# Scores and maxima of an attention stage in four row groups of 32 rows, with the division moved behind the attention

## The chip, the cores and the metric

One core of one Trainium2 chip. The metric is the device time of the whole program in microseconds. The median of three runs of the kernel before is 2633.51 us (2630.73 to 2633.67).

## What is computed

A transformer block with conditioning: x is (2, 2048, 512), 16 heads of 32, MLP width 1024, all in float32. Cut to what matters:

```python
ada = silu(c) @ Wada + bada          # shift, scale and gate for both halves
h = ln(x) * (1 + scale_msa) + shift_msa
q, k, v = h @ Wq + bq, h @ Wk + bk, h @ Wv + bv      # 16 heads of 32
A = softmax(q k^T / sqrt(32))
x = x + gate_msa * ((A v) @ Wo + bo)
h2 = ln(x) * (1 + scale_mlp) + shift_mlp
return x + gate_mlp * (gelu(h2 @ W1 + b1) @ W2 + b2)
```

## The kernel before

Three stages. Stage 1 (to 357 us) makes queries, keys and values in eight chunks of 512 rows. Each query and key is split in two reduced-precision float32 numbers, high and low, and stored in DRAM (q_hi, q_lo, k_hi, k_lo). Stage 3 (from 2180 us) does output projection, norm and MLP in eight blocks of 512 rows; block 0's projection is already done inside the last head.

Stage 2 is the attention: 32 heads g (2 batches of 16), each with 16 key tiles t of 128 keys and four query chunks j of 512 queries. PSUM has eight banks. Per head:

- *Max scores* for head g+1 (max_scores, L1104): 64 matmuls of 96 rows (high and low products below each other) with queries as weights, into three banks in turn. VectorE reduces each to one maximum per query (find_max, L868), then all partial ones (L812); TensorE turns them (transpose_max, L1047), VectorE negates (L818), and one DMA (put_max, L391) lays them as row 96 of the head's queries. Row 96 of the keys is one.
- *Scores* for head g (scores, L1113): 64 matmuls of 97 rows, into three banks in turn. ScalarE takes the exponential of each (probs, L670) into `prob`, a ring of four key tiles.
- *Values* (L1127): for each key tile four matmuls in four column groups of 32, one per query chunk; a float32 matmul is two passes, so eight stand in the trace.
- *Denominators*: GpSimd adds eleven of the sixteen tiles of `prob` in halves (sum_probs, L538, 20 additions), and TensorE sums the other five tiles and GpSimd's result over the partitions (L1118), all accumulated in one bank of its own. ScalarE copies output and denominator (L645, L650); VectorE inverts 128x512 denominators (L874) and multiplies the head's output (L877); SP stores it (store_head, L398).

Each engine runs its own list in order. TensorE's order in a step is: scores of chunks 0 and 1 with max scores between, then the sum of tile t-2 where TensorE has it, values of tile t-1, then scores of chunks 2 and 3 with max scores between. SP's order for head g (stage2, L401) is: load_head for head g+2 (seven DMAs of 256 KB: three pieces of queries, three of keys, values), put_max for head g+1, store_head of head g-1. Buffers of queries, keys, values are three deep. The loop body has three heads. In head 0, twelve weight pieces for stage 3 are loaded and split besides (late, L426, L639, L882). In the last head (31) there are no max scores; block 0 of the attention is loaded in two halves (load_first_oT), split by ScalarE (L689) and VectorE (L896), and projected (first_projection).

In stage 3 a block's attention is loaded (load_oT), split (split_oT, oT_rest) and projected during the block before it (project, after the first of eight mlp2).

## Time and profile before

| | us |
|---|---|
| median of three runs | 2633.51 |
| profiled execution, first to last instruction | 2625.2 |
| TensorE matmuls busy | 2543.3 (97%) |
| weight loads busy (beside the matmuls) | 1482.7 (56%) |
| VectorE busy | 1841.4 (70%) |
| GpSimd busy | 1625.0 (62%) |
| ScalarE busy | 1309.9 (50%) |
| mean granted TensorE clock | 0.989 |
| DMA, mean over the span | 62 GB/s |

A matmul's busy time contains its way through the array, so matmuls overlap in the trace: what one costs is the distance between two starts. PE are matmuls, PEld weight loads, DVE VectorE, ACT ScalarE, POOL GpSimd, SPq SP's queue. "x8" joins neighbours of one kind; in brackets stands the engine's idle time before a row and what ended it. In a row of a stretch the columns are length, busy time with count for PE, PEld, DVE, ACT and POOL, then TensorE's granted clock, DMA share and GB/s.

### The profile page before, as it was taken

The numbers are of one execution on the slowest core, as the hardware profiler recorded it, in microseconds if no ns is written. First come the engines' busy times: TensorE is split into PE (matmuls) and PEld (weight loads), VectorE is DVE, ScalarE is ACT, GpSimd is POOL, SyncE is SP. The second block draws the span as 40 slices with busy tenths as digits, with TensorE's granted clock in tenths as the row PEclk, the third lists the DMA queues.
The fourth block names the chain that finished last, engine by engine and source line by source line (L and its number), as shares of the span: only waits on it lengthen the run. The fifth ranks groups of instructions, "written<-read, shape, count | busy, mean of one in ns | idle before, by whom it ended". The sixth has DMA issues, their size and how long they took to land.

```text
span 2625.2 us, 45742 instructions
## 1 busy us (share of the span) xinstructions
PE 2543.3 (97%) x13208; PEld 1482.7 (56%) x13208; DVE 1841.4 (70%) x2872; ACT 1309.9 (50%) x2429; POOL 1625.0 (62%) x744
## 2 busy tenths in 40 slices
PE   7999899999999999999999999999999979999998
PEld 5788654444444444444444444444444437888887
...
DMA packets 141459, 163.15 MB, mean 62 GB/s; under 512 B 76048, under 2 KB 92944, under 8 KB 134032
## 3 DMA queue, kind: packets, MB, share of 16 engines
...
q14 instruction: 130, 1.06, 0.1%
...
## 4 chain that ended last, share of the span: by engine, by line
PE 93%; DVE 3%; issue 1%; ACT 1%; DMA 1%; SPq 0%; POOL 0%; ACTq 0%; POOLq 0%; DVEq 0%
PE ps L1113 21%; PE ps L1015 20%; PE ps L1104 19%; PE ps L1127 18%; PE ps L1118 7%; PE ps L1248 7%; DVE part_max L868 1%; PE ps L1024 1%; DVE weights_r L882 1%; PE ps L1059 1%; PE ps L1047 0%; DMA work<-v_rows 0%; DVE work L942 0%; ACT work L670 0%; DMA work<-in_x 0%
## 5 line engine op out<-in xcount | busy, mean ns | idle before, releaser
L538 POOL TENSOR_TENSOR work<-work 128x1024 f32<-128x1024 f32 x640 | 1505.7, 2395 | 296.7 <-PE ps L1118 262.7
L868 DVE TENSOR_REDUCE part_max<-ps 128x1 f32<-128x512 f32 x1984 | 1229.0, 682 | 321.3 <-PE ps L1104 320.7
L670 ACT ACTIVATE work<-ps 128x512 f32<-128x512 f32 x2048 | 1070.9, 602 | 697.3 <-PE ps L1113 697.2
L1113 PE MATMUL ps<-acts_r 97*128 97x512 f32 x2048 | 836.4, 418 | 26.0 <-ACT work L670 14.7
L1104 PE MATMUL ps<-acts_r 96*128 96x512 f32 x1984 | 811.3, 409 | 6.8 <-DVE part_max L868 6.7
L1113 PEld LDWEIGHTS ps<-acts_r 97*128 97x128 f32 x2048 | 383.1, 190 | 396.7 <-ACT work L670 308.4
L1127 PE MATMUL ps<-work 128*32 128x512 f32 x4096 | 545.3, 604 | 0.0
L1104 PEld LDWEIGHTS ps<-acts_r 96*128 96x128 f32 x1984 | 375.6, 189 | 263.0 <-DVE part_max L868 182.4
L1015 PE MATMUL ps<-acts_r,weights_r 128*128 128x512 f32 x1536 | 380.3, 397 | 5.7 <-DVE acts_r L790 5.7
L1015 PEld LDWEIGHTS ps<-acts_r,weights_r 128*128 128x128 f32 x1536 | 291.1, 191 | 69.3 <-issue 6.8
L547 POOL TENSOR_TENSOR work<-work,gate_b 128x512 f32<-128x512 f32 x60 | 84.5, 1439 | 214.3 <-DMA work<-in_x 172.8
L1127 PEld LDWEIGHTS ps<-work 128*32 128x32 f32 x4096 | 94.2, 109 | 203.2 <-issue 186.6
L1118 PE MATMUL ps<-work,ones 128*32 128x512 f32 x1536 | 206.4, 610 | 0.0
L505 POOL TENSOR_TENSOR var_eps<-var_eps,mv 128x4 f32<-128x4 f32 x16 | 3.2, 201 | 327.2 <-DVE mv L768 327.2
L713 ACT ACTIVATE work<-ps,b_sb 128x512 f32<-128x512 f32 x64 | 44.1, 690 | 309.7 <-PE ps L1015 309.6
L1248 PE MATMUL ps<-w_r,acts_r 128*128 128x512 f32 x768 | 184.5, 391 | 0.0
L1015 PE MATMUL ps<-weights_r,acts_r 128*128 128x512 f32 x768 | 183.6, 392 | 0.0
L1015 PEld LDWEIGHTS ps<-weights_r,acts_r 128*128 128x128 f32 x768 | 143.7, 188 | 36.9 <-issue 7.0
L1248 PEld LDWEIGHTS ps<-w_r,acts_r 128*128 128x128 f32 x768 | 143.0, 188 | 29.2 <-issue 0.2
L607 ACT ACTIVATE work<-ps,bq_sb 128x512 fp32r<-128x512 f32 x64 | 44.1, 689 | 206.3 <-PE ps L1015 170.9
L922 DVE CAST acts_r<-work 128x512 fp32r<-128x512 f32 x64 | 27.9, 436 | 128.6 <-ACT work L713 128.6
L874 DVE RECIPROCAL bv_rows<-bv_rows 128x512 f32<-128x512 f32 x32 | 106.6, 3331 | 8.0 <-ACT bv_rows L650 8.0
...
## 6 DMA issues: line engine op xcount, KB each, us to landing
work<-in_x SPq DMA_DIRECT2D x16, 1024.0 KB, 5.4
acts_r<-q_hi SPq DMA_DIRECT2D x64, 256.0 KB, 4.8
acts_r<-k_hi SPq DMA_DIRECT2D x64, 256.0 KB, 6.4
q_hi<-work SPq DMA_DIRECT2D x32, 256.0 KB, 2.6
q_lo<-work SPq DMA_DIRECT2D x32, 256.0 KB, 3.3
k_hi<-work SPq DMA_DIRECT2D x32, 256.0 KB, 2.6
k_lo<-work SPq DMA_DIRECT2D x32, 256.0 KB, 3.2
v_rows<-work SPq DMA_DIRECT2D x32, 256.0 KB, 2.0
```

Source lines behind the costliest of these rows:

```text
L538: nc.gpsimd.tensor_tensor(psum_acc[:, at], first, prob[:, t % RING, at], ALU.add).then_inc(add_ok, 1)
L547: nc.gpsimd.tensor_tensor(xc[b][:, t, :], xc[b][:, t, :], gate_b[:, which, b, :], ALU.add).then_inc(done, 1)
L607: nc.scalar.activation(qk_st[:, m % 2, 0, :].bitcast(F32R), ps[:, 2 + m % 4, :], ACT.Identity, bias=bq_sb[:, m // KC, m % KC:m % KC + 1]). ...
L670: nc.scalar.activation(prob[:, t % RING, j * CH:(j + 1) * CH], ps[:, A_BANKS + (u + t * NQ + j) % B_BANKS, :], ACT.Exp, scale=SCALE).then_ ...
L868: nc.vector.tensor_reduce(part_max[:, f // NQ, f % NQ:f % NQ + 1], ps[:, (u + f) % A_BANKS, :], AX.X, ALU.max).then_inc(a_max, 1)
L874: nc.vector.reciprocal(recip[:], recip[:]).then_inc(rec_ok, 1)
L1015: mm = nc.tensor.matmul(o, lhs(s, kk), rhs(r, kk), start=(kk == 0 and s == r), stop=(kk == KC - 1 and s == 1))
L1104: nc.tensor.matmul(ps[:, (u + f) % A_BANKS, :], qs[u][0:M_ROW, f // NQ * P:(f // NQ + 1) * P], ks[u][0:M_ROW, j * CH:(j + 1) * CH], start= ...
L1113: nc.tensor.matmul(ps[:, A_BANKS + (u + t * NQ + j) % B_BANKS, :], ks[u][0:M_ROW + 1, t * P:(t + 1) * P], qs[u][0:M_ROW + 1, j * CH:(j + 1 ...
L1118: mm = nc.tensor.matmul(ps[j * DH:(j + 1) * DH, DEN_BANK, :], ones[:, 0:DH], src(j), start=first, stop=last)
L1127: mm = nc.tensor.matmul(ps[j * DH:(j + 1) * DH, O_BANK, :], v_sb[u][:, t, :], prob[:, t % RING, j * CH:(j + 1) * CH], start=(t == 0), stop ...
L1248: mm = nc.tensor.matmul(ps[:, 4 + t, :], g_r[:, f % 4, s, t * P:(t + 1) * P], w2_r[:, r, f, :], start=(f == 0 and s == r), stop=(f == FB - ...
```

## The change

- Queries and keys are loaded four times, once for each group of 32 partitions: high and low parts of the keys in full (four DMAs of 256 KB each), of the queries one chunk for each group (four of 64 KB each). High parts are three buffers deep, low parts and values two. SP's order for head g is now: high parts of head g+2; the store of a sum; low parts and values of head g+1; store_head; stores of sums, the load of all sums, the store of the reciprocals, and put_max between them.
- A max score multiplies high parts only, 32 rows. A step's four stand in row groups 2, 3, 0, 1. They run two steps ahead of the head (LEAD), so the maxima of head g+1 are complete after step 13 of head g. Head 0 has two steps' worth more.
- A score of chunk r is four accumulating matmuls in row group r and bank 3+r: high by high, low by high, high by low, and a row of minus ones by the row of maxima. The chunks' parts are interleaved.
- The maxima are turned by VectorE in 32x32 squares and laid into one row per group by 16 DMAs; TensorE waits for them before the first tile's last part.
- GpSimd adds ten tiles. The six other tiles and GpSimd's result are summed over partitions each into a max bank; ScalarE copies each into one buffer `sums`, SP stores it. The seven are loaded back spread over all partitions, VectorE adds and inverts them (128x16), SP stores the reciprocals.
- The head's output is stored undivided. At the output projection the reciprocals are loaded (16 DMAs a block) and multiplied on: by VectorE for block 0, by GpSimd for the others.
- The last block of w2 is loaded and split in the last head, since its place holds queries before. The loop body has six heads, the loop four rounds, and heads 25 to 30 stand unrolled.

```diff
--- before.py
+++ after.py
@@ constants @@
-NBUF = 3
+HI_BUF, TWO = 3, 2
+PERIOD = 6
-POOL_TILES = [0, 1, 2, 3, 5, 6, 7, 9, 10, 11, 12]
+POOL_TILES = [0, 1, 3, 4, 6, 7, 9, 10, 12, 13]
+ND = len(PE_TILES) + 1
+EXPS = 4
+LEAD = 2
+EXTRA_AT = (3, 8)
+A_BANKS, S_BANK, O_BANK = 3, 3, 7
+LOADS_HI, LOADS_LO, LOADS_0 = 8, 9, 6
+MAX_PIECES = 4
...
@@ def _(sp): @@
+            def load_k(dst, src, g, done):
+                for r in range(NQ):
+                    sp.dma_start(dst[r * DH:(r + 1) * DH, :].bitcast(F32), src[1][bass.ds(g * DH, DH), :]).then_inc(done, 16)
+            def load_q(dst, src, g, done):
+                for r in range(NQ):
+                    sp.dma_start(dst[r * DH:(r + 1) * DH, :].bitcast(F32), src[0][bass.ds(g * DH, DH), r * CH:(r + 1) * CH]).then_inc(done, 16)
+            def load_hi(g, u):
+                load_q(q_hi[u], qk_hi, g, hi_in[u])
+                load_k(k_hi[u], qk_hi, g, hi_in[u])
...
+                for w in range(MAX_PIECES):
+                    for r in range(NQ):
+                        row = m_row[u][r * DH:r * DH + 1, :].bitcast(F32).rearrange("o (s q) -> o s q", q=P)
+                        sp.dma_start(row[:, :, w * DH:(w + 1) * DH],
+                                     max_T[w * DH + r * TT:w * DH + (r + 1) * TT, :]).then_inc(maxT_in, 16)
...
+            def store_sums(i, g, uses):
+                for d, _, _, n in uses:
+                    n = i * (PERIOD * ND) + n
+                    sp.wait_ge(sums_ok, n)
+                    sp.dma_start(sums_dram[bass.ds(g * ND + d, 1), :].rearrange("o (r q) -> (o r) q", q=CH), sums[0:P:DH, :]).then_inc(sums_out, 16)
+            def load_sums(g):
+                sp.wait_ge(sums_out, 16 * ND * (g + 1))
+                sp.dma_start(sums_c[:], sums_dram[bass.ds(g * ND, ND), :].rearrange("n (p x) -> p n x", x=NT)).then_inc(sums_in, 16)
+            def store_rec(g):
+                sp.wait_ge(rec_ok, g + 1)
+                sp.dma_start(rec_dram[bass.ds(g, 1), :].rearrange("o (p x) -> (o p) x", x=NT), rec_c[:]).then_inc(rec_out, 16)
...
+                if loads:
+                    sp.wait_ge(b_mm, g * FILLS)
+                    load_hi(g + 2, (k + 2) % HI_BUF)
+                sums_of((0,))
+                if load_next:
+                    sp.wait_ge(pv_mm, START + g * NT)
+                    sp.wait_ge(b_mm, g * FILLS)
+                    load_lo(g + 1, (k + 1) % TWO)
+                    load_v(g + 1, (k + 1) % TWO)
+                store_head(g - 1, (k - 1) % TWO)
+                sums_of(range(1, 5))
+                load_sums(g - 1)
+                sums_of(range(5, 9))
+                store_rec(g - 1)
+                sums_of(range(9, NT - 1))
+                if load_next:
+                    put_max(g + 1, (k + 1) % TWO)
+                sums_of((NT - 1,))
...
+            sp.wait_ge(a_max, FILLS)
+            load_q(q_hi[0], qk_hi, 0, hi_in[0])
             put_max(0, 0)
-            store_v(NCHUNK - 1, *ORDER[NCHUNK - 1], range(2, TT))
+            load_hi(1, 1)
...
+            def load_rec(b, c, dst):
+                for k in range(KC):
+                    for r in range(NQ):
+                        src = rec_dram[bass.ds(b * H + c * NQ, NQ), k * CH + r * P:k * CH + (r + 1) * P]
+                        src = src.rearrange("g (o q) -> o g q", o=1).broadcast_to((DH, NQ, P))
+                        sp.dma_start(dst[k][r * DH:(r + 1) * DH, :].rearrange("d (g q) -> d g q", q=P), src).then_inc(rec_in, 16)
...
+            sp.wait_ge(oT_ok, 2)
+            sp.dma_start(w2_st, w2[FF - P:FF, :]).then_inc(w2_last_in, 16)
+            load_sums(G - 2)
...
+            load_sums(G - 1)
+            store_rec(G - 1)
+            sp.wait_ge(rec_out, 16 * G)
+            load_rec(1, 0, rec)
...
@@ def _(pool): @@
+                pool.wait_ge(rec_in, (n + 1) * (16 * KC * NQ))
+                pool.wait_ge(oT_in, n * 16 + 32)
+                for blk in range(KC):
+                    nc.gpsimd.tensor_tensor(oTf[:, blk, :], oTf[:, blk, :], rec[blk], ALU.mult).then_inc(oT_ok, 1)
...
@@ def _(act): @@
+            def take_sums(i, g, uses):
+                for d, bank, _, n in uses:
+                    if d < ND - 1:
+                        act.wait_ge(pv_mm, START + g * NT + PE_TILES[d] + 1)
+                    else:
+                        act.wait_ge(den_mm, START + g + 1)
+                    if n > 1:
+                        act.wait_ge(sums_out, 16 * (i * (PERIOD * ND) + n - 1))
+                    nc.scalar.activation(sums, ps[:, bank, :], ACT.Copy).then_inc(sums_ok, 1)
...
@@ def _(dve): @@
+            def transpose_max(g):
+                dve.wait_ge(max_ok, g + 1)
+                if not isinstance(g, int) or g:
+                    dve.wait_ge(maxT_in, g * (16 * MAX_PIECES))
+                nc.vector.transpose(max_T[:], row_max[:]).then_inc(maxT_ok, 1)
...
+            def denominators(g):
+                dve.wait_ge(sums_in, 16 * (g + 1))
+                if not isinstance(g, int) or g:
+                    dve.wait_ge(rec_out, 16 * g)
+                nc.vector.tensor_reduce(den_c[:], sums_c[:].rearrange("p n x -> p x n"), AX.X, ALU.add).then_inc(den_ok, 1)
+                dve.wait_ge(den_ok, g + 1)
+                nc.vector.reciprocal(rec_c[:], den_c[:]).then_inc(rec_ok, 1)
...
+            def normalise_first(half):
+                dve.wait_ge(oT_in, 16 * half + 16)
+                if half == 0:
+                    dve.wait_ge(rec_in, 16 * KC * NQ)
+                for k in range(2):
+                    nc.vector.tensor_tensor(tmp3[:, k, :], tmp3[:, k, :], rec0[:, 2 * half + k, :], ALU.mult).then_inc(oT_ok, 1)
...
@@ def _(pe): @@
+            def bank_free(i, before):
+                if before:
+                    kind, n = before
+                    if kind == "M":
+                        pe.wait_ge(a_max, i * (PERIOD * FILLS) + n)
+                    else:
+                        pe.wait_ge(sums_ok, i * (PERIOD * ND) + n)
+            def max_tile(i, u, q, r, use):
+                bank, before, _ = use
+                bank_free(i, before)
+                at = slice(r * DH, (r + 1) * DH)
+                nc.tensor.matmul(ps[:, bank, :], q_hi[u][at, q // NQ * P:(q // NQ + 1) * P],
+                                 k_hi[u][at, q % NQ * CH:(q % NQ + 1) * CH], start=True, stop=True).then_inc(a_mm, 1)
+            def score_part(i, k, t, r, part):
+                g, u, w = i * PERIOD + k, k % HI_BUF, k % TWO
+                if part == 0 and (t or k):
+                    pe.wait_ge(exp_ok, START + g * (NT * EXPS) + t * EXPS + r - EXPS + 1)
+                if part == 3 and t == 0:
+                    pe.wait_ge(maxT_in, (g + 1) * (16 * MAX_PIECES * NQ))
+                at = slice(r * DH, (r + 1) * DH)
+                keys = slice(t * P, (t + 1) * P)
+                o = ps[:, S_BANK + r, :]
+                if part == 0:
+                    nc.tensor.matmul(o, k_hi[u][at, keys], q_hi[u][at, :], start=True, stop=False)
+                elif part == 1:
+                    nc.tensor.matmul(o, k_lo[w][at, keys], q_hi[u][at, :], start=False, stop=False)
+                elif part == 2:
+                    nc.tensor.matmul(o, k_hi[u][at, keys], q_lo[w][at, :], start=False, stop=False)
+                else:
+                    row = slice(r * DH, r * DH + 1)
+                    nc.tensor.matmul(o, minus_r[row, :], m_row[w][row, :], start=False, stop=True).then_inc(b_mm, 1)
...
+            def take_sums(i, k, uses):
+                for d, bank, before, _ in uses:
+                    bank_free(i, before)
+                    if d < ND - 1:
+                        sums_of(lambda j: prob[:, PE_TILES[d] % RING, j * CH:(j + 1) * CH], bank).then_inc(pv_mm, 1)
+                    else:
+                        pe.wait_ge(add_ok, START + (i * PERIOD + k + 1) * (NADD * HALVES))
+                        sums_of(lambda j: psum_acc[:, j * CH:(j + 1) * CH], bank).then_inc(den_mm, 1)
...
+                for t, step in enumerate(A_USES[k]):
+                    ahead = 1 + q // per_head
+                    u = (k + ahead) % HI_BUF
+                    if step["max"] and (k == 0 and t == 0 or q == per_head):
+                        pe.wait_ge(hi_in[u], (nth(i, k + ahead, HI_BUF) + 1) * (16 * LOADS_HI))
+                    if step["extra"]:
+                        for r, use in zip((2, 3, 0, 1), step["extra"]):
+                            max_tile(i, u, q % per_head, r, use)
+                        q += 1
+                    score_part(i, k, t, 0, 0)
+                    score_part(i, k, t, 1, 0)
+                    for r, use in zip((2, 3), step["max"][:2]):
+                        max_tile(i, u, q % per_head, r, use)
+                    for part in range(1, 4):
+                        score_part(i, k, t, 0, part)
+                        score_part(i, k, t, 1, part)
+                        score_part(i, k, t, 2, part - 1)
+                        score_part(i, k, t, 3, part - 1)
+                    for r, use in zip((0, 1), step["max"][2:]):
+                        max_tile(i, u, q % per_head, r, use)
+                    score_part(i, k, t, 2, 3)
+                    score_part(i, k, t, 3, 3)
+                    if step["max"]:
+                        q += 1
+                    if t:
+                        values(i, k, t - 1)
+                    elif k:
+                        values(i, k - 1, NT - 1)
+                    take_sums(i, k if t > 1 else k - 1, step["sums"])
                     if t in between:
                         between[t]()
```

## Rows read from the trace of the kernel before

**Rows 1.** The page: TensorE's share, and the chain that ended last by line
```profile
PE 2543.3 (97%) x13208; PEld 1482.7 (56%) x13208; DVE 1841.4 (70%) x2872; ACT 1309.9 (50%) x2429; POOL 1625.0 (62%) x744
...
PE ps L1113 21%; PE ps L1015 20%; PE ps L1104 19%; PE ps L1127 18%; PE ps L1118 7%; PE ps L1248 7%; DVE part_max L868 1%; PE ps L1024 1%; DVE weights_r L882 1%; PE ps L1059 1%; PE ps L1047 0%; DMA work<-v_rows 0%; DVE work L942 0%; ACT work L670 0%; DMA work<-in_x 0%
```
**Rows 2.** Groups by line (line, engine, form, count, busy us, mean ns)
```profile
L874 DVE RECIPROCAL bv_rows<-bv_rows 128x512 f32<-128x512 f32 x32 | 106.6, 3331 | 8.0 <-ACT bv_rows L650 8.0
...
L547 POOL TENSOR_TENSOR work<-work,gate_b 128x512 f32<-128x512 f32 x60 | 84.5, 1439 | 214.3 <-DMA work<-in_x 172.8 <-DVE work L773 41.4
...
L818 DVE TENSOR_SCALAR neg_max<-ps 16x128 fp32r<-16x128 f32 x32 | 8.9, 279 | 22.8 <-PE ps L1047 22.8
```
**Rows 3.** SP's queue, put_max (L391): start us, us; heads 1, 31; all 32
```profile
422.67 0.52 SPq L391 DMA_DIRECT2D acts_r<-neg_max  x1
...
2088.83 0.52 SPq L391 DMA_DIRECT2D acts_r<-neg_max  x1
...
L391 SPq DMA_DIRECT2D acts_r<-neg_max x32: 512/518/621, 354.3 to 2088.8; - x32
...
DMA to landing us min/median/max: 1.8/1.8/1.9
```
**Rows 4.** Timeline of TensorE, one step and a step's start (start us, us, what)
```profile
1055.29 1.06 PE L1127 MATMUL ps<-work 128*32 128x512 f32 x8
...
1056.62 0.40 PE L1104 MATMUL ps<-acts_r 96*128 96x512 f32 x1
...
1058.03 0.40 PE L1104 MATMUL ps<-acts_r 96*128 96x512 f32 x1
1058.36 1.06 PE L1118 MATMUL ps<-work,ones 128*32 128x512 f32 x8
1059.24 1.04 PE L1127 MATMUL ps<-work 128*32 128x512 f32 x8
```
**Rows 5.** SP's queue, one head's output stores
```profile
1037.28 1.89 SPq L398 DMA_DIRECT2D attention_T<-work  x4
```
**Rows 6.** Timelines: VectorE and GpSimd in a middle head, ScalarE in the last head
```profile
1053.52 3.08 DVE L868 TENSOR_REDUCE part_max<-ps 128x1 f32<-128x512 f32 x5 [0.34 <-PE ps L1104]
...
1042.95 47.06 POOL L538 TENSOR_TENSOR work<-work 128x1024 f32<-128x1024 f32 x20 [8.07 <-PE ps L1118]
...
2159.47 2.06 ACT L670 ACTIVATE work<-ps 128x512 f32<-128x512 f32 x4 [0.60 <-PE ps L1113]
```
**Rows 7.** Timeline of weight loads (PEld): into column groups, and full width
```profile
1055.29 0.16 PEld L1127 LDWEIGHTS ps<-work 128*32 128x32 f32 x8 [0.24 <-issue]
...
100.29 0.53 PEld L1003 LDWEIGHTS ps<-tmp 128*128 128x128 f32 x4
```
**Rows 8.** A stretch with a head's loads (last three: PEclk, DMA share, GB/s)
```profile
1044.00:1052.00 8.00, 8.00 (x44) 4.40 (x42) 6.88 (x12) 6.17 (x13) 7.87 (x4) 1.00 1.05 214
```
**Rows 9.** DMA issues: count, KB each, median us from issue to landing
```profile
work<-in_wada SPq DMA_DIRECT2D x5, 1024.0 KB, 5.6
...
gate<-in_wv SPq DMA_DIRECT2D x1, 1024.0 KB, 14.6
...
bv_rows<-in_bv SPq DMA_DIRECT2D x1, 256.0 KB, 12.3
```
**Rows 10.** TensorE after a wait, the stretch behind it, and twelve us of the last head
```profile
379.46 0.50 PE L1104 MATMUL ps<-acts_r 96*128 96x512 f32 x1 [1.40 <-DVE part_max L868]
...
380.60:384.00 3.40, 3.40 (x16) 1.29 (x19) 3.40 (x3) 1.83 (x4) 3.34 (x3) 0.50 0.13 49
2148.00:2160.00 12.00, 11.02 (x55) 3.80 (x51) 1.44 (x7) 8.79 (x18) 11.21 (x7) 1.00 0.00 0
```
**Rows 11.** TensorE's first matmul of head 0
```profile
357.48 0.47 PE L1113 MATMUL ps<-acts_r 97*128 97x512 f32 x1 [0.83 <-issue]
```
**Rows 12.** A wait in the last head; first MLP matmuls; block 1's projection
```profile
ACT acts_r L689 <- DMA tmp<-attention_T: 11.1, 1, 11.1
...
2180.10 8.45 PE L1015 MATMUL ps<-acts_r,weights_r 128*128 128x512 f32 x36 [1.83 <-DVE acts_r L790]
...
2193.92 3.34 PE L1015 MATMUL ps<-weights_r,acts_r 128*128 128x512 f32 x14
```

More of the change, by code:

```diff
@@ L124, in block_kernel @@
         gf = view(work, 3584, 2, CH)
+        rec = [view(work, at, CH) for at in (2560, 3072, 4608, 5120)]
         assert STEP_ROOT in POOL_TILES
@@ L430, in _ @@
                     stored(NCHUNK)
-                    load_head(2, 2)
+                    load_v(1, 1)
+                    load_hi(2, 2)
+                    load_lo(1, 1)
+            for t in range(len(late), NT - 1):
+                store_sums(0, 0, A_USES[0][t]["sums"])
             put_max(1, 1)
-            with sp.Fori(0, G // NBUF - 1) as i:
-                for k in range(1, NBUF + 1):
-                    stage2(i * NBUF + k, k % NBUF, True)
+            store_sums(0, 0, A_USES[0][NT - 1]["sums"])
+            with sp.Fori(0, ROUNDS) as i:
+                for k in range(1, PERIOD + 1):
+                    head(i, k)
             def heads_stored(n):
-                for u in range(NBUF):
-                    sp.wait_ge(o_out[u], START + 16 * NQ * len(range(u, n, NBUF)))
+                for u in range(TWO):
+                    sp.wait_ge(o_out[u], START + 16 * NQ * len(range(u, n, TWO)))
             def rows_oT(b, c):
@@ L1117, in denominators, with sums_of, values @@
+            def sums_of(src, bank):
                 for j in range(NQ):
-                    mm = nc.tensor.matmul(ps[j * DH:(j + 1) * DH, DEN_BANK, :], ones[:, 0:DH], src(j), start=first, stop=last)
+                    mm = nc.tensor.matmul(ps[j * DH:(j + 1) * DH, bank, :], ones[:, 0:DH], src(j), start=True, stop=True)
                 return mm
-            def values(g, u, t):
-                pe.wait_ge(exp_ok, START + g * (NT * NQ) + (t + 1) * NQ)
-                if t == 0 and not (isinstance(g, int) and g == 0):
+            def values(i, k, t):
+                g = i * PERIOD + k
+                pe.wait_ge(exp_ok, START + g * (NT * EXPS) + (t + 1) * EXPS)
+                if t == 0 and k:
@@ L1190, in _ @@
             pe.wait_ge(v_ok, START + NCHUNK * TT)
[L1191 to L1192 removed]
+            pe.wait_ge(a_max, FILLS)
+            pe.wait_ge(hi_in[0], 16 * LOADS_HI)
+            head(0, 0)
             nc.disable_value_cache = True
[L1194 to L1197 removed]
+            with pe.Fori(0, ROUNDS) as i:
+                for k in range(1, PERIOD + 1):
+                    head(i, k)
@@ L1198, in _ @@
             nc.disable_value_cache = False
+            for g in range(AFTER, G - 1):
+                head(0, g)
             def project_tile(n, t):
```

420 lines of the change are left out of this document (226 added, 194 removed).

## Prediction

> **What bounds the kernel now.** I read the page's shares first, then its groups by line, then single steps of the timeline. TensorE is busy 97% of the span, and three of its lines in the attention stage are most of the chain that ended last: scores (L1113) 21%, max scores (L1104) 19%, values (L1127) 18% [rows 1]. (L1015, the products of the other stages, isn't touched.) The queue's put_max rows give the time of a head: (2088.83 - 422.67)/30 = 55.5 us [rows 3]. A step of a head is seen in [rows 4]: eight 512-column score or max matmuls, one each 0.233 us, then the values. From one values group to the next are 3.07 us, so all that is not those eight costs 3.07 - 8 x 0.233 = 1.20; a step that also sums its tile (L1118) costs 0.88 more. A head is 128 x 0.233 + 16 x 1.20 + 6 x 0.88 = 54.4 of the 55.5 us. The other engines have room: per 55.5 us a head costs VectorE 64 maxima at 0.62 (five stand in 3.08) = 39.7 and 3.3 of reciprocal, ScalarE 64 exponentials at 0.49 (four in 2.06) = 31.4, GpSimd 20 additions in 47.1 [rows 2, 6].
>
> **What the change takes off TensorE.** A max score of 96 rows becomes one of 32; four stand in four row groups and four banks. A score becomes four accumulating parts (high x high, low x high, high x low, minus the maximum), each in its own row group. If four row groups work at the same time, a step has five rounds in place of eight matmuls. The trace before has no row groups. The nearest rows are the values: eight passes into four column groups, each shown as about 0.6 us, are through in 1.0 us, and their eight weight loads begin within 0.16 us [rows 4, 7]. I take full overlap, a round at 0.233 (upper bound: none at all, 4 x 0.233). Then TensorE's own work is 80 x 0.233 + 19.2 + 7 x 0.88 = 44.0 us a head, 10.4 less. The Trainium skill ("TensorEngine Tiling (Array Packing)", Key Properties) says that different tiles load weights and multiply in parallel, which would be this value.
>
> GpSimd goes from 20 additions to 18 (42.4 us); VectorE loses the reciprocal of 3.3 and keeps 39.7. ScalarE copies seven sums and one output, 8 x 0.49, 35.3 in all. None of these is above 44. What sets the head is who waits for whom:
>
> **1. The four score banks.** Bank r of step t+1 must wait for exponential r of step t, and the third and fourth row group enter a round after the first two; the TensorE queue is in order, so the first bank's last two parts stand behind the fourth bank's first. After the fourth exponential: 0.16 to the matmul, one round, then 0.43 until the exponential starts. Before, in the last head, which has no max scores, the same kind of loop shows as four exponentials in 2.07 and 0.60 idle [rows 6]. Here it is 2.07 + 0.16 + 0.233 + 0.43 = 2.90 us for a step without a sum (9 of them). A step with a sum (7) is TensorE's: 5 x 0.233 + 1.20 + 0.88 = 3.25. Together 26.1 + 22.8 = 48.9 us. After a sum, a max matmul waits for its copy (the sums use the max banks): 0.5 a head in step 1.
>
> **2. The maximum's way to its row.** Removed: one transpose on TensorE, one negation, one DMA. Added: a VectorE transpose and 16 DMAs. SP issues one each 0.46 us (four in 1.89), and one such DMA lands 1.8 us after its issue [rows 3, 5]. The search runs two steps ahead: the last maximum is reduced about 2.2 us into step 13's later rounds, maxima and transpose (the negation's 0.28 [rows 2] as its price; the transpose is in no row) end at 2.75, and the row is complete at 2.75 + 0.1 + 15 x 0.46 + 1.8 + 0.2 = 11.75. The first bank's last part of the next head is due at 2.90 + 2.90 + 3.25 + 0.23 = 9.28. TensorE stands 2.5 us each head, with values, sums and max scores queued behind that wait.
>
> **3. The partial sums' way out.** ScalarE has one buffer for them, so a copy waits until the last store has landed. The store after step 1 stands in SP's queue behind load_lo and load_v (9 issues) and store_head (4), and on the rings behind their data. A head loads 2.8 MB where it loaded 1.8; the 8 us stretch of a head load shows 214 GB/s [rows 8], so high and low parts take 12 us, values and output 3. Counted from step 14, the high parts are issued from 7.9 and their data run to 15; the row of maxima is there at 8.7; the low parts are issued from 13.3 (after step 0's sum), their data and the values' run to 23, the output's and the store's to 24.5; step 3's copy wants it at 21.8 and the exponentials of step 4 queue behind it. That is 2.4 us, or 1.6 after point 4 has moved the copy later. Whether a small store waits behind bulk is seen in the start of the kernel: 1 MB loads issued close behind each other land 5.6 us after their issue (median of five) and then 14.6, and the smaller one issued behind them after 12.3 [rows 9]. At the low bound (1.8 us, as put_max alone) this wait is zero.
>
> **4. TensorE's clock.** In the trace before, a stand of 1.40 us (at 378) is soon followed by 3.4 us at a granted clock of 0.50 (1.2 GHz in place of 2.4) [rows 10]. The last head's steps, 11.02 us busy of 12, kept 1.00 [rows 10], and the new steps' stands are no longer than theirs. The waits of points 2 and 3 are as long, so I expect two such stretches a head: in steps 0 and 1, which TensorE sets, half of 3.4 = 1.7 us; in steps 4 and 5, which have 0.9 us of room each, about 1.1. Low bound 0.
>
> A head: 48.9 + 0.5 + 2.5 + 1.7 + 1.6 + 1.1 = 56.3 us, 0.8 more than before; times 30 = +23 us. TensorE's gain of 10.4 goes into waits: its saving is real and all of it is spent.
>
> **5. The two ends.** Start: head 0 may begin only with head 1's keys. SP issues 4 query loads, then 16 for the maximum (found at about 354.3, when put_max was issued before [rows 3]), then 8 more: 354.5 + 24 x 0.46 = 365.5, and some 4.5 us for the last 256 KB to land, 370 against 357.5 [rows 11]; with a slow clock behind it +14.5. Last head: its first block of attention is divided on VectorE before ScalarE may split it (ScalarE stands 11.1 us for that block already [rows 12]) +3; w2's last piece is split between step 8's exponentials and the residual, +4; 12 steps at 2.90 in place of 2.67 +3; x's norm waits one tile longer +1. Block 1's projection began 13.8 us after the first MLP matmul (2193.92 - 2180.10) [rows 12]; now the last sum must be copied (0.6), stored (2.3), loaded spread over the partitions (3.5, more packets), added and inverted (0.5), stored (2.3), and 16 loads issued and landed (9.2), multiplied on GpSimd (four at 1.44 [rows 2]) and split (1.2): about 26 us. +12 and 2 of slow clock. The later blocks' divisions are loaded a block ahead and lie beside TensorE's work; uncovered, each would cost 5.8. Ends: +39.5 us.
>
> **The sum.** The profiled run is 2625.2 us, the median 2633.5, 8.3 more (I add that). 2633.5 + 23 + 39.5 = 2696 us.
>
> **Rivals.** *Shorter waits (faster than before).* If the small stores are not held by the bulk, point 3 and its slow stretch go: 53.6 a head, 30 x -1.9 = -57, 2616. If short stands do not lower the clock either, 51.9 a head: 30 x -3.6 = -108, 2565. For it: put_max's 1.8 us [rows 3], and that the load of before has room between its bursts; against: the landings of [rows 9] and the clock of [rows 10]. It decides at 54.2 us a head, where 30 heads pay for the ends. Chance 0.26.
> *Row groups share the weight load.* Full-width loads one behind the other take 0.53 us for four, 0.11 from start to start [rows 7]. If the four row groups take turns at it, a round is 0.45: steps of 3.45 and 4.33, 61.4 a head, the row of maxima waits 0.7, the clock stays: 62.5, 30 x 7 = +210, 2883. A round of 0.30 would give 51.8 + 0.5 + 2.1 + 1.7 + 1.3 + 1.0 = 58.4, 30 x 2.9 = +87, 2760. Its mechanism is the same, a part of the overlap missing; for it: no row shows row groups; against: the eight loads within 0.16. Chance 0.20 for both. The Trainium skill ("TensorE: Matmul & The Clock Gate", Measured speedup vs the span model) has four tiles of 32 rows at 3.07 times one after another; an estimate from that is 4 x 0.233/3.07 = 0.30.
> *It does not overlap at all.* 20 x 0.233 + 1.20 a step: 100 us a head, near 4000. Chance 0.03.
> *My forecast* of two waits a head holds 0.51, with its own range 2650 to 2745 (an issue of 0.37 or 0.56 instead of 0.46 moves 15 issues by 1.5 us).
> The Trainium skill ("TensorEngine Tiling (Array Packing)", PSUM Bottleneck) says tiling speeds up the matmuls and not what empties PSUM. Point 1 agrees with it by rows: the exponentials' loop sets nine steps of 16.
>
> **Numbers.** 0.2% (5 us) is about what a measurement can tell. Faster by more: 0.26 from the short waits and 0.01 = 0.27. Within: 0.05, between the cases. Slower: 0.68. The range goes from the short-wait case's middle to the partly overlapping rounds and above, 2580 to 2840.
>
> **What would show it.** Right: heads of 56 us; max and score matmuls of 32 rows starting four together, rounds 0.23 apart; four exponentials in 2.07, 0.8 idle; at step 0 TensorE stands 2 to 3 us for the max row's DMA; ScalarE's third sums copy waits for a DMA; PEclk under 1 in the slices of the stage; TensorE idle 12 us before head 0 and before block 1's projection. Wrong: rounds further apart than 0.3, no DMA wait ahead of step 0, a sums store that lands in 2 us behind load_v, or heads under 54.2 us.

## The result: 11% slower, and the profile after

The kernel after takes 2918.3 us (median of four runs, 2914.9 to 2922.0) against 2632.7 for the kernel before, a ratio of 1.109 (interval 1.107 to 1.111). The forecast was 2696, in a range up to 2840: the sign was right, the size far off. The profiled run spans 2919.5 us, 294.3 more than before.

The page of the kernel after (shares; chain by engine and by line; three groups: line, engine, operation, count | busy us, mean ns | idle before):

```profile
PE 2552.5 (87%) x19544; PEld 1366.5 (47%) x19544; DVE 1756.7 (60%) x2878; ACT 1420.8 (49%) x2622; POOL 1505.1 (52%) x706
...
PE 63%; SPq 21%; DMA 5%; issue 4%; DVE 4%; ACT 3%; POOL 0%; ACTq 0%; DVEq 0%; POOLq 0%
PE ps L1245 17%; PE ps L1374 13%; SPq L489 9%; PE ps L1353 7%; SPq L496 6%; PE ps L1490 6%; PE ps L1364 5%; PE ps L1339 4%; PE ps L1355 3%; PE ps L1360 3%; PE ps L1357 2%; SPq L470 2%; SPq L466 2%; DMA partial_sums<-work 2%; DVE part_max L1069 2%
...
L1360 PE MATMUL ps<-acts_r,minus_r 1*128 1x512 f32 x1024 | 240.9, 470 | 65.0 <-DMA acts_r<-max_T 65.0
L1360 PE MATMUL ps<-m_odd,minus_r 1*128 1x512 f32 x1024 | 234.6, 460 | 57.3 <-DMA m_odd<-max_T 57.3
...
L838 ACT ACTIVATE work<-ps 128x512 f32<-128x512 f32 x224 | 133.9, 598 | 224.9 <-DMA partial_sums<-work 166.8
```

Before, three TensorE lines made up most of the chain [rows 1]. Now 21% of it is SP's queue: the row of maxima (L489, put_max) has 9%, the output stores (L496, store_head) 6%, loads (L466, L470) and small stores the rest. The two waits at the right are the two places the prediction named: TensorE at the row of maxima (122 us in all) and ScalarE's copies at the stores of the sums (167 us).

Where the 294.3 us are, by the same landmarks as in [rows 3, 11, 12]. TensorE's start of head 0, the first put_max in head 0, the one 30 heads later, the first MLP matmul and block 1's projection after:

```profile
375.12 0.79 PE L1353 MATMUL ps<-acts_r 32*128 32x512 f32 x2 [18.56 <-DVE work L1002]
...
453.92 2.49 SPq L489 DMA_DIRECT2D m_odd<-max_T  x4
...
2353.76 0.61 SPq L489 DMA_DIRECT2D m_odd<-max_T  x1
...
2458.68 8.47 PE L1245 MATMUL ps<-acts_r,weights_r 128*128 128x512 f32 x36 [1.38 <-ACT work L838]
...
2485.20 2.07 PE L1245 MATMUL ps<-weights_r,acts_r 128*128 128x512 f32 x4 [12.54 <-DVE acts_r L1121]
```

| stretch | before | after | more | forecast |
|---|---|---|---|---|
| to the first matmul of head 0 | 357.5 | 375.1 | +17.6 | +14.5 |
| from there to the first put_max | 65.2 | 78.8 | +13.6 | 0 |
| 30 heads: (2353.76 - 453.92)/30 = 63.3 each | 1666.2 | 1899.8 | +233.7 | +23 |
| to the first MLP matmul | 91.3 | 104.9 | +13.6 | +11 |
| to block 1's projection | 13.8 | 26.5 | +12.7 | +14 |
| the rest | | | +3.1 | 0 |

The ends are nearly as forecast; the heads are not. One head of the kernel after on SP's queue (start, length from first to last of the joined issues), then ScalarE in the same head. L858 are the exponentials, L838 copies of sums, L827 the output; step 0 starts at 1034.60:

```profile
1022.78 9.91 SPq L489 DMA_DIRECT2D acts_r<-max_T  x16
1032.97 0.59 SPq L504 DMA_DIRECT2D partial_sums<-work  x1
1033.85 1.92 SPq L470 DMA_DIRECT2D acts_r<-q_hi  x4
1035.86 2.76 SPq L466 DMA_DIRECT2D acts_r<-k_hi  x4
1040.12 0.61 SPq L504 DMA_DIRECT2D partial_sums<-work  x1
1041.32 1.71 SPq L470 DMA_DIRECT2D acts_r<-q_lo  x4
1043.12 1.77 SPq L466 DMA_DIRECT2D acts_r<-k_lo  x4
1045.09 0.40 SPq L477 DMA_DIRECT2D work<-v_rows  x1
1045.69 6.22 SPq L496 DMA_DIRECT2D attention_T<-work  x4
1052.18 3.08 SPq L504 DMA_DIRECT2D partial_sums<-work  x2
```

```profile
1034.60 2.06 ACT L858 ACTIVATE work<-ps 128x512 f32<-128x512 f32 x4 [5.34 <-PE ps L1360]
...
1046.80 2.06 ACT L858 ACTIVATE work<-ps 128x512 f32<-128x512 f32 x4 [0.82 <-PE ps L1360]
1053.95 0.60 ACT L838 ACTIVATE work<-ps 128x512 f32<-128x512 f32 x1 [5.08 <-DMA partial_sums<-work]
1054.44 2.19 ACT L858 ACTIVATE work<-ps 128x512 f32<-128x512 f32 x4
1059.39 2.06 ACT L858 ACTIVATE work<-ps 128x512 f32<-128x512 f32 x4 [2.76 <-PE ps L1360]
1062.48 2.06 ACT L858 ACTIVATE work<-ps 128x512 f32<-128x512 f32 x4 [1.02 <-PE ps L1360]
1065.05 0.60 ACT L838 ACTIVATE work<-ps 128x512 f32<-128x512 f32 x1 [0.51 <-PE ps L1364]
1066.06 2.07 ACT L858 ACTIVATE work<-ps 128x512 f32<-128x512 f32 x4 [0.41 <-PE ps L1360]
1068.96 2.07 ACT L858 ACTIVATE work<-ps 128x512 f32<-128x512 f32 x4 [0.84 <-PE ps L1360]
1071.85 2.07 ACT L858 ACTIVATE work<-ps 128x512 f32<-128x512 f32 x4 [0.82 <-PE ps L1360]
```

Undisturbed steps (from 1066) are the forecast's: 2.90 us, four exponentials in 2.07, idle 0.8. The two stands (stretches in which an engine waits), 5.34 and 5.08 us, are not. TensorE, the rounds of such a step, and the granted clock after each stand (last columns: PEclk, DMA share, GB/s):

```profile
1065.16 0.40 PE L1355 MATMUL ps<-acts_r 32*128 32x512 f32 x2
1065.17 0.40 PE L1353 MATMUL ps<-acts_r 32*128 32x512 f32 x2
...
1065.63 0.39 PE L1360 MATMUL ps<-acts_r,minus_r 1*128 1x512 f32 x2
1065.64 0.40 PE L1357 MATMUL ps<-w_r,acts_r 32*128 32x512 f32 x2
```

```profile
1033.60:1040.40 6.80, 6.63 (x40) 2.94 (x44) 2.16 (x4) 3.15 (x6) 0.00 (x0) 0.50 0.67 169
...
1053.90:1061.00 7.10, 6.40 (x40) 2.39 (x40) 3.76 (x6) 4.27 (x9) 4.68 (x2) 0.52 0.08 9
```

Four matmuls in four row groups start within 0.01 us, and 1065.16 to 1065.63 are two rounds, 0.23 each. The four groups overlap in full. Behind both stands of this head the clock is 0.50, the 1.2 GHz level, for about 6.8 us. It isn't always so long. From the first exponential of head 1 to that of head 31, 64 stretches at 0.50 begin in the trace, 39 of 6.8 us and 25 of 3.4. A stand of 4.35 us at the row of maxima, as long as the one before 1033.77, has 3.4 us behind it here:

```profile
780.38 0.59 PE L1360 MATMUL ps<-acts_r,minus_r 1*128 1x512 f32 x2 [4.35 <-DMA acts_r<-max_T]
...
781.00:784.40 3.40, 3.40 (x20) 0.85 (x18) 1.29 (x2) 1.98 (x4) 0.00 (x0) 0.50 0.46 121
784.40:787.80 3.40, 3.31 (x40) 1.39 (x36) 2.39 (x4) 2.79 (x6) 0.00 (x0) 1.00 1.02 243
```

### The profile page after: what moved, and what is told of

Its sections match the earlier page's. It is cut to its first block, busy times and chain, and to the rows that moved or that the text cites. A ratio compares the mean times of both kernels' runs of the same rounds, so it can differ in the third digit from the quotient of the medians.

```text
span 2919.5 us, 59447 instructions
## 1 busy us (share of the span) xinstructions
PE 2552.5 (87%) x19544; PEld 1366.5 (47%) x19544; DVE 1756.7 (60%) x2878; ACT 1420.8 (49%) x2622; POOL 1505.1 (52%) x706
## 4 chain that ended last, share of the span: by engine, by line
PE 63%; SPq 21%; DMA 5%; issue 4%; DVE 4%; ACT 3%; POOL 0%; ACTq 0%; DVEq 0%; POOLq 0%
PE ps L1245 17%; PE ps L1374 13%; SPq L489 9%; PE ps L1353 7%; SPq L496 6%; PE ps L1490 6%; PE ps L1364 5%; PE ps L1339 4%; PE ps L1355 3%; PE ps L1360 3%; PE ps L1357 2%; SPq L470 2%; SPq L466 2%; DMA partial_sums<-work 2%; DVE part_max L1069 2%
## 5 line engine op out<-in xcount | busy, mean ns | idle before, releaser
L710 POOL TENSOR_TENSOR work<-work 128x1024 f32<-128x1024 f32 x576 | 1352.8, 2386 | 784.5 <-PE ps L1364 431.5
L858 ACT ACTIVATE work<-ps 128x512 f32<-128x512 f32 x2048 | 1060.0, 603 | 563.1 <-PE ps L1360 561.9
L1374 PE MATMUL ps<-work 128*32 128x512 f32 x4096 | 613.4, 674 | 0.0
L1339 PE MATMUL ps<-acts_r 32*128 32x512 f32 x1344 | 397.6, 503 | 103.9 <-ACT work L838 85.9
L1353 PE MATMUL ps<-acts_r 32*128 32x512 f32 x1408 | 357.3, 494 | 33.8 <-DVE work L1002 18.6
L1353 PEld LDWEIGHTS ps<-acts_r 32*128 32x128 f32 x1408 | 154.8, 198 | 414.7 <-ACT work L858 340.6
L1355 PE MATMUL ps<-acts_r 32*128 32x512 f32 x1408 | 310.0, 431 | 0.0
L1360 PE MATMUL ps<-acts_r,minus_r 1*128 1x512 f32 x1024 | 240.9, 470 | 65.0 <-DMA acts_r<-max_T 65.0
L1360 PE MATMUL ps<-m_odd,minus_r 1*128 1x512 f32 x1024 | 234.6, 460 | 57.3 <-DMA m_odd<-max_T 57.3
L1339 PEld LDWEIGHTS ps<-acts_r 32*128 32x128 f32 x1344 | 186.6, 197 | 181.3 <-ACT work L838 105.1
L1364 PE MATMUL ps<-work,ones 128*32 128x512 f32 x1792 | 257.9, 651 | 0.0
L838 ACT ACTIVATE work<-ps 128x512 f32<-128x512 f32 x224 | 133.9, 598 | 224.9 <-DMA partial_sums<-work 166.8
L1339 PE MATMUL ps<-acts_r,w_r 32*128 32x512 f32 x640 | 187.5, 506 | 44.5 <-ACT work L838 42.5
L1357 PE MATMUL ps<-w_r,acts_r 32*128 32x512 f32 x1024 | 218.1, 446 | 0.0
L1357 PE MATMUL ps<-acts_r 32*128 32x512 f32 x1024 | 215.1, 442 | 0.0
```

The lines of the kernel that those rows point to most:

```text
L710: nc.gpsimd.tensor_tensor(psum_acc[:, at], first, prob[:, t % RING, at], ALU.add).then_inc(add_ok, 1)
L858: nc.scalar.activation(prob[:, t % RING, j * CH:(j + 1) * CH], ps[:, S_BANK + j, :], ACT.Exp, scale=SCALE).then_inc(exp_ok, 1)
L1339: nc.tensor.matmul(ps[:, bank, :], q_hi[u][at, q // NQ * P:(q // NQ + 1) * P], k_hi[u][at, q % NQ * CH:(q % NQ + 1) * CH], start=True, sto ...
L1353: nc.tensor.matmul(o, k_hi[u][at, keys], q_hi[u][at, :], start=True, stop=False)
L1355: nc.tensor.matmul(o, k_lo[w][at, keys], q_hi[u][at, :], start=False, stop=False)
L1357: nc.tensor.matmul(o, k_hi[u][at, keys], q_lo[w][at, :], start=False, stop=False)
```

## The experiments

All times are medians of four runs. For each kernel the steps of a head are given as the time from the first exponential of a step to that of the next, mean over heads 1 to 30 of its profiled run; steps 5 to 14 differ little and only one kind stands here.

| kernel | us | step 15 | 0 | 1 | 2 | 3 | 4 | later, no sum | head | head 0 |
|---|---|---|---|---|---|---|---|---|---|---|
| after | 2918.3 | 8.31 | 5.49 | 3.87 | 3.09 | 7.08 | 4.64 | 2.91 | 63.3 | 87.3 |
| e1_max4 | 2757.1 | 3.77 | 3.92 | 6.32 | 4.19 | 5.50 | 3.50 | 2.91 | 58.2 | 84.4 |
| e2_lead4 | 2842.1 | 6.10 | 4.64 | 4.86 | 3.43 | 6.42 | 4.18 | 2.91 | 60.5 | 86.2 |
| e3_values_later | 2791.1 | 8.38 | 5.49 | 3.90 | 3.15 | 4.42 | 3.30 | 2.91 | 59.3 | 87.7 |
| e4_sums_first | 2750.9 | 8.36 | 5.57 | 3.72 | 2.96 | 3.51 | 2.91 | 2.91 | 57.7 | 87.2 |
| e5_both | 2670.1 | 3.73 | 3.78 | 6.36 | 4.26 | 3.68 | 2.91 | 2.91 | 55.4 | 84.4 |
| e6_spread | 2552.5 | 3.78 | 3.97 | 3.77 | 2.97 | 3.46 | 2.91 | 2.91 | 51.6 | 87.3 |
| e7_lag | 2592.3 | 3.87 | 3.89 | 3.78 | 3.02 | 3.58 | 2.95 | 2.96 | 52.6 | 88.6 |
| e9_max_last | 2545.3 | 3.78 | 3.74 | 3.77 | 2.97 | 3.44 | 2.91 | 2.91 | 51.3 | 84.2 |
| e8_lag_max_last | 2535.2 | 3.81 | 3.69 | 3.77 | 2.97 | 3.45 | 2.71 | 2.73, 2.90 | 50.9 | 81.6 |
| e10_split_later | 2535.0 | 3.74 | 3.70 | 3.78 | 2.94 | 3.44 | 2.91 | 2.91 | 51.3 | 73.0 |
| e11_all | 2530.4 | 3.89 | 3.79 | 3.76 | 2.97 | 3.44 | 2.72 | 2.73, 2.90 | 51.0 | 75.7 |

The kernel before has 55.5 and 67.6 in the last two columns. The theory at the start: the 7.8 us a head are two waits on SP's queue, each with its slow clock. The rivals: the loads' data, or a cost of the row groups themselves.

**Row of maxima by 4 DMAs.**

```diff
-for r in range(NQ):
-    row = m_row[u][r * DH:r * DH + 1, :]...
-    sp.dma_start(row[:, :, w * DH:(w + 1) * DH], max_T[w * DH + r * TT:w * DH + (r + 1) * TT, :])
+rows = m_row[u][0:P:DH, :].bitcast(F32).rearrange("r (s q) -> r s q", q=P)
+sp.dma_start(rows[:, :, w * DH:(w + 1) * DH], max_T[w * DH:w * DH + NT, :])
```

> The row of maxima is laid by 4 DMAs (four rows each) in place of 16. Theory (a head of the changed kernel is 50.0 us of steps, a stand of 4.9 for this row at step 0, 2.7 for the slow clock behind it, 4.2 for ScalarE's copy in step 3 and 2.2 for the slow clock behind that): 12 issues of 0.62 us less, the stand at step 0 and its slow clock go, the second wait stays. 56 us a head in place of 63.3, and 7 us at the start: about 2690 us. Rival (the row isn't what step 0 waits for, or the clock is low for another reason): 2770 or more.

2757.1 us, ratio 1.047 (1.043 to 1.051). The stand at step 0 is gone: steps 15 and 0 lose 6.1 us together. But step 1 gains 2.5 and step 2 gains 1.1, and the copies' wait for the DMA of the sums is longer than before the edit, 199.8 us in 60 waits. SP and ScalarE:

```profile
1098.40 0.61 SPq L503 DMA_DIRECT2D partial_sums<-work  x1
...
1104.06 6.45 SPq L495 DMA_DIRECT2D attention_T<-work  x4
```

```profile
1103.58 0.60 ACT L837 ACTIVATE work<-ps 128x512 f32<-128x512 f32 x1 [4.15 <-DMA partial_sums<-work]
```

Step 0's store, issued at 1098.40 right behind the eight loads of the high parts, has landed only by 1103.58. In the kernel after, step 0 ran at half clock and its store went out 6.3 us after the first of those loads (1033.85 to 1040.12); now it is 4.2. So the time lies between the two expectations, nearer to the rival's, for a reason that neither had named: the stand and its slow clock had covered another wait.

**Maxima four steps ahead instead of two.**

```diff
-LEAD = 2
-EXTRA_AT = (3, 8)
+LEAD = 4
+EXTRA_AT = (3, 6, 9, 12)
```

> Maxima run four steps ahead instead of two, the 16 DMAs stay. Theory: the row is asked for 5.8 us earlier, which is more than the stand of 4.9, so it goes as with 4 DMAs, with the clock behind it: 56 us a head, 2700 us. Rival (SP's issuing is full, and what is moved ahead comes back elsewhere): the gain is under half of that, 2810 or more.

2842.1 us, ratio 1.080 (1.078 to 1.081): on the rival's side, for a reason that neither had named. The maxima are complete two steps earlier, but put_max stands in SP's list behind the store of step 12's sums:

```profile
1118.65 0.54 SPq L504 DMA_DIRECT2D partial_sums<-work  x1
1119.24 9.91 SPq L489 DMA_DIRECT2D acts_r<-max_T  x16
```

The 16 issues begin right behind that store, and step 0's exponentials start at 1130.7. Only half of TensorE's wait goes (from 122 to 63 us in all).

**Values loaded after the first stores.**

```diff
     load_lo(g + 1, (k + 1) % TWO)
-    load_v(g + 1, (k + 1) % TWO)
 store_head(g - 1, (k - 1) % TWO)
 sums_of(range(1, 5))
+if load_next:
+    load_v(g + 1, (k + 1) % TWO)
```

> Only SP's order: the values' load (2048 pieces of 128 bytes) goes behind the output store and the stores of steps 1 and 3. Theory A (its pieces hold up SP's issue: the four output stores took 6.2 us to issue behind it, 1.9 before): the stores issue in 1.9, step 3's copy waits under 1 us, its slow clock goes: 57 us a head, 2726 us. Theory B (the 1.3 MB of low parts on the rings hold the store, as predicted): the copy still waits 3 us, 2860 or more.

2791.1 us, ratio 1.060 (1.058 to 1.061).

```profile
1130.49 1.92 SPq L496 DMA_DIRECT2D attention_T<-work  x4
```

The four output stores are issued in 1.92 us instead of 6.22, and step 3 falls from 7.08 to 4.42. The load of the values is one DMA, but of 2048 pieces of 128 bytes, and output stores issued right behind it are held: 4.73 to 7.49 us for the four in heads 1 to 30 of the kernel after, 1.87 to 2.90 here, where the low parts' 256 KB loads stand before them. That it is the number of pieces, and nothing else about this load, was not tried. Step 3 keeps 1 us over the 3.44 of an undisturbed step with a sum: step 1's store still stands behind the low parts' eight issues and the output. The time lies midway between the expectations, with 2.7 of the 3.6 us of step 3 on the side of the first.

**Output stores and step 1's sums ahead of both loads.**

```diff
 sums_of((0,))
+store_head(g - 1, (k - 1) % TWO)
+sums_of((1,))
 if load_next:
     ...
     load_lo(g + 1, (k + 1) % TWO)
     load_v(g + 1, (k + 1) % TWO)
-store_head(g - 1, (k - 1) % TWO)
-sums_of(range(1, 5))
+sums_of(range(2, 5))
```

> Only SP's order: the output store and the store of step 1's sums go ahead of low parts and values. Both theories of the second wait: it goes with its slow clock, 57 us a head, 2726 us. Rival (the wait moves to step 6, whose copy needs step 3's store, now behind low parts and values): 2800 or more.

2750.9 us, ratio 1.045 (1.043 to 1.046). Nearer to the first theory (2726) than to its rival. Steps 1 to 14 are at their base with the clock at 1.00; only the stand for the row is left. Point 3 with its slow clock was 63.3 - 57.7 = 5.6 us a head.

**The edits of e1_max4 and e4_sums_first together.** There is no other edit.

> The edits of e1_max4 and e4_sums_first together: the row of maxima by 4 DMAs, and the output stores and step 1's sums ahead of the two bulk loads. Theory A (SP's queue issues one after the other, and a wait that is taken away uncovers what stood in its shadow): the steps 15 and 0 shrink from 8.36 + 5.57 to 3.77 + 3.92 as in e1_max4, but step 0's store of the sums stands behind the eight loads of load_hi, which e4_sums_first hid in the stand for the row, so step 1 grows from 3.72 to 6.3. A head is 57.7 - 3.6 = 54.1 us, the time about 2750 - 30 x 3.6 - 7 (the first head's row) = 2635 us. Theory B (the two waits are separate costs and their gains add up, 167 + 169 us): 2918 - 336 = 2585 us.

2670.1 us, ratio 1.014 (1.011 to 1.016). The separate gains (161 and 167 us) don't add up to 328 but to 248; a third wait has come out at step 1, as the first theory said (6.36 us against 6.3). It was 35 us slower than that theory's 2635, because the clock falls again in step 2 (4.26 us, mean granted clock 0.64 over it). e1_max4 had shown that step already (4.19), and the theory left it out.

```profile
1071.36 0.60 SPq L503 DMA_DIRECT2D partial_sums<-work  x1
```

```profile
1076.21 0.60 ACT L838 ACTIVATE work<-ps 128x512 f32<-128x512 f32 x1 [4.43 <-DMA partial_sums<-work]
```

Here it isn't the issue: the store goes out at 1071.36 and has landed 4.85 us later, behind the data of the high parts.

**SP's order spread over the head,** with the 4 DMAs of e1_max4.

```diff
+sums_of((0,))
+store_head(g - 1, (k - 1) % TWO)
+sums_of((1,))
 load_hi(g + 2, (k + 2) % HI_BUF)
-sums_of((0,))
+sums_of(range(2, 5))
+load_sums(g - 1)
 load_lo(g + 1, (k + 1) % TWO)
+sums_of(range(5, 7))
 load_v(g + 1, (k + 1) % TWO)
-store_head(g - 1, (k - 1) % TWO)
-sums_of(range(1, 5))
-load_sums(g - 1)
-sums_of(range(5, 9))
+sums_of(range(7, 9))
 store_rec(g - 1)
```

> The 4 DMAs, and SP's order within a head is: sums of step 0, output stores, sums of step 1, load_hi, sums of step 3, load_sums, load_lo, sums of step 6, load_v, store_rec, sums of 9 and 12, row of maxima, sums of 15. No store of sums then stands behind a load that was issued in the same step. Theory A (all that a head takes over its 50.3 us of loop is the order of issue on SP's queue, and the slow clock that follows a stand): 51 to 51.5 us a head instead of 63.3, so 2918 - 30 x 12 - 7 = 2550 us, 2535 to 2575, below the kernel before; granted clock 1.00 in nearly every step, and the copies' wait for the sums' DMA under 20 us in all. Theory B (the loads' own transfers, not their issue, delay the small stores, or the clock falls for another reason): the waits move to steps 3 and 6 and a head stays above 54 us, 2630 us or more.

2552.5 us, ratio 0.968 (0.967 to 0.970): faster than the kernel before. It moves the same 211 MB; only the number of issues for the row and the order differ from the kernel after, and from e5_both only the order, which is worth 118 us. Among its 60 longest groups of waits none is of the copies for the DMA of the sums. The chain by engine, from its page, and a head's stretch (columns as above):

```profile
PE 88%; DVE 3%; DMA 3%; ACT 3%; issue 2%; SPq 1%; POOL 0%; ACTq 0%; DVEq 0%; POOLq 0%
```

```profile
1021.00:1073.00 52.00, 49.65 (x492) 20.54 (x488) 40.10 (x68) 37.72 (x72) 42.18 (x18) 1.00 0.32 66
```

SP's queue has left the chain (1%), the clock is 1.00 through the head, and TensorE is busy for 49.65 of 52.00 us.

**Six rounds a step instead of seven, then the maximum tiles last.** In e7_lag row groups 2 and 3 run two rounds behind in steps without a sum; in e9_max_last and e8_lag_max_last the maximum tiles of row groups 0 and 1 come after the last score matmuls instead of before them.

```diff
+lag = 1 if step["sums"] else 2
-for part in range(1, 4):
+for part in range(1, 4 + lag):
     ...
-    score_part(i, k, t, 2, part - 1)
+    score_part(i, k, t, 2, part - lag)
```

> As e6_spread, and in the 9 steps without a sum the third and fourth row group run two rounds of matmuls behind the first and second instead of one, so that a step has six rounds between the release of its first and its last bank instead of being tied to the bank three exponentials back at 2.90 us. Theory (point 1 of the prediction: the loop over the four score banks sets 2.90 us): with the later banks asked for one round later, the step is 2.07 + 0.16 + 0.43 = 2.66 us, 9 x 0.24 = 2.2 us a head less, 65 us less in all than e6_spread. Rival (the matmuls, the reductions of the maxima or the value product bind beside the loop at 2.9): within 15 us of e6_spread.

2592.3 us, ratio 0.984 (0.982 to 0.985): 40 us slower than e6_spread, where the theory had 65 faster. TensorE in e7_lag:

```profile
1031.61 0.76 PE L1341 MATMUL ps<-acts_r 32*128 32x512 f32 x2
1031.87 0.50 PE L1359 MATMUL ps<-acts_r 32*128 32x512 f32 x2
1032.21 0.40 PE L1362 MATMUL ps<-m_odd,minus_r 1*128 1x512 f32 x2
1032.53 1.07 PE L1376 MATMUL ps<-work 128*32 128x512 f32 x8
```

The maximum tiles (L1341) wait for a bank that VectorE still reads; the last two rounds and the values stand behind them in TensorE's list. The waits of such tiles were 87.6 us in 250 times in e6_spread. In e7_lag and then in e8_lag_max_last (us, times, longest) they were:

```profile
PEld ps L1341 <- DVE part_max L1071: 154.0, 458, 3.5
```

```profile
PEld ps L1341 <- DVE part_max L1071: 78.8, 236, 3.1
```

```diff
-for r, use in zip((0, 1), step["max"][2:]):
-    max_tile(i, u, q % per_head, r, use)
 score_part(i, k, t, 2, 3)
 score_part(i, k, t, 3, 3)
+for r, use in zip((0, 1), step["max"][2:]):
+    max_tile(i, u, q % per_head, r, use)
```

> As e6_spread, but the maximum tiles of row groups 0 and 1 are asked for after the last score matmuls of row groups 2 and 3 instead of before them, so that TensorE's queue doesn't hold those behind a bank that VectorE still reads. Theory A: in e6_spread the loop of 2.90 us goes exponential 3 (ends), the first matmul of row group 3, the last of row group 0, exponential 0, and the maximum tiles are not in it; steps of the 30 heads stay within 0.05 us, only head 0, where VectorE's splitting of late weights holds the tiles, gains up to 10 us: 2540 to 2553 us. Rival: the tiles' wait for VectorE is in the loop, a step gains 0.1 us or more, 2510 us or less.

2545.3 us, within its theory A's range. Without the lag the tiles' place is worth 7 us at most; the interval (0.965 to 0.969) overlaps that of e6_spread. The theory had put the gain into head 0 alone; 3.1 us are there, and step 0 of the others falls by 0.23 (3.97 to 3.74).

> As e7_lag, with the same move of the two maximum tiles behind the last score matmuls. In e7_lag the steps were 2.96 and 3.58 us instead of 2.66 and 3.44. Theory A (with two rounds of lag the maximum tile's wait for VectorE stands before the last two rounds of the third and fourth row group and before the value product, so TensorE's own order sets the step): freed of it, one of the two steps between sums loses up to 0.33 us, 51.55 + 1.05 - 5 x 0.33 = 50.9 us a head, about 2540 us. Theory B (TensorE's chain of rounds, value product and sums is as long as the step by itself): within 10 us of e7_lag's 2592 us.

2535.2 us, ratio 0.962 (0.960 to 0.964); a head of 50.9 as its theory A says. ScalarE in e8_lag_max_last, a step after a sum and the next:

```profile
1025.01 2.07 ACT L860 ACTIVATE work<-ps 128x512 f32<-128x512 f32 x4 [0.43 <-PE ps L1362]
1027.72 2.07 ACT L860 ACTIVATE work<-ps 128x512 f32<-128x512 f32 x4 [0.64 <-PE ps L1362]
1030.62 2.06 ACT L860 ACTIVATE work<-ps 128x512 f32<-128x512 f32 x4 [0.84 <-PE ps L1362]
```

2.71, then 2.90. So the loop of point 1 is real, since asking for the later banks a round later shortens a step, but only one of two: why the other keeps 2.90 was not tried. Head 0 takes the rest of the 10 us to e9_max_last (84.2 to 81.6).

**Head 0.** On VectorE, in head 0:

```diff
-{LATE_STEP + k: lambda k=k: split_late_lo(k) ...
+{LATE_STEP + 1 + k: lambda k=k: split_late_lo(k) ...
```

> As e9_max_last, and in the first head VectorE subtracts each late weight piece one step later, so that it doesn't wait for ScalarE's split of the same step. Theory A (head 0's steps of 4 to 5 us are the ring exponentials, ScalarE's split, VectorE's subtraction, its reduction, the maximum tile, the next scores): head 0 falls from about 87 us to 70 to 75 us, 12 us or more less in all than e9_max_last. Rival (SP's issue of the late pieces, 12.60 us for three in the trace of after, sets head 0): within 4 us of e9_max_last.

2535.0 us, 10 less than e9_max_last where the theory had 12 or more; head 0 falls from 84.2 to 73.0, inside its 70 to 75. The rival is out. So 11.2 of head 0's excess of 16.6 us over the 67.6 before went with the ring through ScalarE's split and VectorE's subtraction. Slow clock is part of it: over head 0 the granted clock is 0.92 in the kernel before, 0.71 after, 0.72 in e9_max_last and 0.83 here.

Both lines of edits together:

> The edits of e8_lag_max_last and of e10_split_later together. Theory A (they lie in different stretches, the lag in the steps 4 to 14 of heads 1 to 30, the later subtraction in head 0): a head of 50.9 us as in e8_lag_max_last and a head 0 near 71 us, against 81.6 in e8_lag_max_last: 2535 - 10 = 2525 us, 2515 to 2530. Rival (e8_lag_max_last's shorter head 0 is already the same gain): 2533 to 2537 us.

2530.4 us, ratio 0.959 (0.958 to 0.961), the fastest here. Head 0 is 75.7, not 71, so the gains add up in part; at 5 us between it and its two parents I call this undecided.

## Why the prediction was wrong, by its own steps

**Overlap of the row groups: right.** Rounds are 0.23 us apart. The rivals with a part of the overlap missing are out, although the time lies near their 2883. A time alone would have confirmed the wrong mechanism. The Trainium skill ("TensorE: Matmul & The Clock Gate", Measured speedup vs the span model) has 3.07 times for four tiles; the rows here show four times, and the measurement decides.

**Point 1: right, with a small miss.** 2.90 us as forecast. A step with a sum is 3.44, not 3.25: 9 x 2.91 + 7 x 3.44 = 50.3 us, 0.9 over the 48.9 + 0.5.

**Point 2: right place, half the size.** An issue was priced at 0.46 from the output stores [rows 5], while the old put_max itself stood at 0.518 in [rows 3]. The 16 issues took 9.91 us (0.62 each) where 7.4 was assumed. TensorE stood 4.35 us where 2.5 was forecast; ScalarE's exponentials, which follow at the low clock, come 4.9 us late (5.34 instead of 0.41). The price of the issue covers the whole miss: 2.5 + 15 x 0.16 = 4.9.

**Point 3: the failed step.** The forecast had 24.5 - 21.8 us, written as 2.4 though it is 2.7, and 1.6 after point 4. Step 3's copy waits 5.08 us, and the step takes 7.64 (1046.80 to 1054.44) instead of 3.44: 4.2 us, not 1.6. The forecast let the store land late behind the loads' data; its data were through within 1.8 us of the issue (1052.18 to 1053.95). The step that fails is "9 issues, and store_head (4)" at a flat price: the 9 issues were rightly priced (1041.32 to 1045.49), but the four took 6.22 us behind the load of the values, 4.3 more than [rows 5]. e3_values_later shows which load it was. The data mechanism exists too, in another place: behind the high parts a store lands after 4.85 us (e5_both), hidden in the kernel after.

**Point 4: right, too small.** 2.7 and 2.2 us in the head shown instead of 1.7 and 1.1. The forecast took 3.4 us at half clock for each stand, from the one stand of 1.40 us in [rows 10]; of the 64 stretches here 39 were 6.8 us long, some 11.5 us a head in all. What decides between the two lengths stays open: stands of 4.35 us had either behind them.

A head is then 50.3 + 4.9 + 2.7 + 4.2 + 2.2 = 64.3, for 64.0 from 1022.78 to 1086.81, the first issue of the next put_max; the mean of 30 is 63.3. Terms that were each sized at a half or two thirds make 7 us a head, and 30 heads 210 us.

**Point 5: right** within about 3 us for each end. Most of the start's 3.1 us is the issue price again: the 16 of head 0 took 10.03 us instead of 7.4. No row had shown the 3.5 us for the load of the sums; it landed in 2.2 (median of 32). Head 0's 13.6 us were not in the sum: the late weights' splits now close a ring with the maxima and the scores, as e10_split_later shows.

**The range** ended at 2840 although the low bounds of points 2 to 4 had been carried and their upper ones not. [rows 3] show an issue of 0.621 at most, which is 15 x 0.16 = 2.4 us more in point 2 and 13 x 0.16 = 2.1 in point 3: 4.5 us a head, 135 in all, and 2831 before any more slow clock. With the extra clock measured here (1.0 and 1.1 us a head) it would have been 2894, still short of 2918.

**The pivot** of 54.2 us a head held: e5_both with 55.4 is slower than before, e6_spread with 51.6 faster. So the faster rival's outcome was possible, through an order of the queue rather than through kinder hardware. That its 51.9 us a head is nearly e6_spread's 51.6 is luck. Its sum still has 2.5 us for the row of maxima, and e6_spread has no such wait among its 60 longest groups; there the loop takes 0.9 us more than forecast, and steps 15, 0 and 1 take 3.8 to 4.0 instead of 3.44.
